# Graph attention on one core: 16-bit projection operands, turns of h between the units of k, and the transposes of the probabilities moved next to the scores

## The reference

```python
h = jnp.maximum(_layernorm(x, axis=-1), 0.0)
q = _split_heads(h @ Wq + bq)
k = _split_heads(h @ Wk + bk)
v = _split_heads(h @ Wv + bv)
scores = jnp.einsum('bhqd,bhkd->bhqk', q, k) / jnp.sqrt(HD)
scores = scores + beta * adj_e
scores = jnp.where(adj_e > 0, scores, -9000000000000000.0)
probs = jax.nn.softmax(scores, axis=-1)
out = jnp.einsum('bhqk,bhkd->bhqd', probs, v)
return x + out.transpose(0, 2, 1, 3).reshape(B, N, D)
```

## Time and profile before

| | |
|---|---|
| median of 3 runs | 1162.26 us (1161.06 to 1162.73) |
| the profiled execution | 1160.99 us, span 1159.1 us |
| busy of the span | PE 94%, PE weight loads 78%, DVE 84%, ACT 77%, POOL 50% |
| granted PE clock, mean | 0.974 of full speed |

### The profile page before, as it was taken

One profiled execution on the slowest core, in us unless ns is written; L12 is line 12 of the kernel. 1 busy time (PEld: TensorE's weight loads), 2 busy tenths in 40 slices (PEclk: granted clock), 3 DMA queues, 4 the chain that ended last, 5 costly groups with the idle time before them and its releaser, 6 DMA issues. The chain is left out here.

```text
span 1159.1 us, 33776 instructions
## 1 busy us (share of the span) xinstructions
PE 1089.7 (94%) x10959; PEld 902.9 (78%) x10959; DVE 972.2 (84%) x4343; ACT 891.0 (77%) x2343; POOL 578.6 (50%) x756
## 2 busy tenths in 40 slices
PE   4899999999999999999999999999999999999986
PEld 2778878888878888787888887888888788888764
DVE  6578888888888888898888888888889888888865
ACT  2377888788787888787888878788877888887865
POOL 3735464454555454546545455545454554545331
PEclk9999999999999999999999999999999999999965
DMA  4444434554434455444455443445544444543320
GB/s 145 116 123 123 110 105 123 140 147 126 120 98 123 130 140 136 120 111 113 119 137 147 130 116 100 122 128 139 145 115 109 114 119 134 147 126 98 98 70 28
DMA packets 91038, 138.79 MB, mean 120 GB/s; under 512 B 15600, under 2 KB 66288, under 8 KB 90864
## 3 DMA queue, kind: packets, MB, share of 16 engines
q1 hardware_dynamic: 90336, 135.85, 43.7%
q10 hardware_dynamic: 528, 0.79, 0.2%
HBM read 35.91 MB, written 25.17 MB: 53 GB/s over the span
## 5 line engine op out<-in xcount | busy, mean ns | idle before, releaser
L523 ACT ACTIVATE probs<-biased,neg_max 128x128 f32<-128x128 f32 x1536 | 491.9, 391 | 222.8 <-DVE neg_max L638 186.0
L435 PE MATMUL ps_p<-hT,w 128*128 128x512 f32 x1728 | 527.1, 423 | 5.2 <-DVE qT L619 2.5
L644 DVE TENSOR_TENSOR pT<-ps_t,pT 128x512 f16<-128x512 f32 x384 | 262.9, 685 | 141.3 <-ACT pT L548 141.0
L334 POOL TENSOR_TENSOR on<-on,xb 128x384 f32<-128x384 f32 x128 | 129.2, 1009 | 471.8 <-DVE on L659 392.9
L638 DVE CUSTOM_DVE_ANT_0 biased<-ps_s,mask 128x128 f32<-128x128 f32 x1536 | 352.0, 285 | 6.3 <-PE ps_s L456 4.3
L435 PEld LDWEIGHTS ps_p<-hT,w 128*128 128x128 f32 x1728 | 294.2, 192 | 53.4 <-DVE hT L609 7.3
L435 PE MATMUL ps_p<-w,hT 128*128 128x384 f32 x1152 | 270.2, 357 | 30.4 <-DVE hT L609 30.4
L464 PE MATMUL ps_t<-ident,probs 128*128 128x128 f32 x1536 | 237.8, 279 | 3.1 <-ACT probs L523 1.5
L464 PEld LDWEIGHTS ps_t<-ident,probs 128*128 128x128 f32 x1536 | 193.9, 143 | 43.8 <-ACT probs L523 7.1
L548 ACT ACTIVATE pT<-ps_t 128x512 f16<-128x512 f32 x384 | 220.5, 574 | 1.2 <-PE ps_t L464 1.2
L435 PEld LDWEIGHTS ps_p<-w,hT 128*128 128x128 f32 x1152 | 186.8, 189 | 37.6 <-DVE hT L609 37.5
(11 more groups left out here) (62 smaller groups left out, 1034.9 us busy)
## 6 DMA issues: line engine op xcount, KB each, us to landing
q_st<-qT SPq DMA_DIRECT2D x384, 96.0 KB, 2.2
k_st<-kT SPq DMA_DIRECT2D x384, 96.0 KB, 2.2
out<-on SPq DMA_DIRECT2D x128, 192.0 KB, 2.1
xs<-in_x SPq DMA_DIRECT2D x31, 768.0 KB, 4.8
adjs<-in_adj SPq DMA_DIRECT2D x32, 256.0 KB, 5.1
xs<-in_x ACTq DMA_DIRECT2D x1, 768.0 KB, 7.6
k_st<-in_L_gnn_Wq SPq DMA_DIRECT2D x1, 576.0 KB, 5.9
k_st<-in_L_gnn_Wk SPq DMA_DIRECT2D x1, 576.0 KB, 9.2
```

Of the source, the lines that this page charges most:

```text
L334: pool.tensor_tensor(on[:, j % 2, :], on[:, j % 2, :], xb[:, par, j, :], ALU.add).then_inc(added, 1)
L435: mm = pe.matmul(dst, stationary, moving, start=m == 0, stop=m == MMS - 1)
L523: act.activation(probs[:, odd, i, :], biased[:, odd, i, :], ACT.Exp, bias=neg_max[:, odd, i:i + 1], scale=-1.0).then_inc(exp_done, 1)
L644: dve.tensor_tensor(pT[:, odd, 1], ps_t[odd][:].rearrange("p (h q) -> p h q", q=N), pT[:, odd, 0], ALU.subtract).then_inc(p_low_done, 1)
```

## The change

1. `w` and `hT` become FP16. To keep small values within the format, h is made smaller by SHRINK = 4 (in the variance that goes into the reciprocal root) and the weights are made larger by 4.
2. The units become q0 q1 q2 k0 turn0 k1 turn1 k2 turn2 v0 v1 v2 v3.
3. The projection work of a slot is one piece, and `turn_probs` comes ahead of it, right behind the scores.
4. On DVE, `moments` and `variance` run for two graphs in slot 0 and two in slot 1, no longer one in each of slots 0 to 3.
5. On POOL, `rstd_of` and `normalise` move ahead of `add_x(s - 2, 2)` and `add_bias(s, 2)`.

```diff
+SHRINK = 4.0
...
-    UNITS = ([("q", c) for c in range(CH)] + [("k", c) for c in range(CH)]
-             + [("v", 0), ("v", 1), ("turn", 0), ("v", 2), ("turn", 1), ("v", 3), ("turn", 2)])
+    UNITS = ([("q", c) for c in range(CH)] + [(kind, c) for c in range(CH) for kind in ("k", "turn")]
+             + [("v", j) for j in range(G)])
...
+    QK_AT = {o: [u for u in UNITS if u[0] in "qk"].index(unit) for o, unit in enumerate(UNITS) if unit[0] in "qk"}
...
-    HALVES = 2 * SLOTS
-    PIECES = [[] for _ in range(HALVES)]
+    PIECES = [[] for _ in range(SLOTS)]
...
-        w = sb("w", [P, 2, CH, 3 * D], F32R)
+        w = sb("w", [P, 2, CH, 3 * D], FP16)
...
-        hT = sb("hT", [P, 2, 2, CH, TOK], F32R)
+        hT = sb("hT", [P, 2, 2, CH, TOK], FP16)
...
-                pool.tensor_scalar(var_eps[:], mean_var[:, :, 1], EPS, None, ALU.add).then_inc(eps_added, 1)
+                pool.tensor_scalar(var_eps[:], mean_var[:, :, 1], SHRINK * SHRINK, SHRINK * SHRINK * EPS, ALU.mult,
+                                   ALU.add).then_inc(eps_added, 1)
...
+                if 0 <= s <= STEPS - 2:
+                    rstd_of(s + 1)
+                    normalise(s + 1, 1 - par)
                 if older:
                     add_x(s - 2, par, 2)
                 if proj:
                     add_bias(s, par, 2)
-                if 0 <= s <= STEPS - 2:
-                    rstd_of(s + 1)
-                    normalise(s + 1, 1 - par)
...
                     if scored:
                         scores(*scored, (u - LAG) % 2)
-                    if proj:
-                        piece(s, par, 2 * u, ahead)
                     if turning:
                         turn_probs(turning[0], (u - LAG - 1) % 2)
                     if proj:
-                        piece(s, par, 2 * u + 1, ahead)
+                        piece(s, par, u, ahead)
                     if valued:
                         values_of(*valued, (u - LAG) % 2)
...
-                act.activation(w[:, 0, :, W_COLS[n]], w_raw[:, :, W_COLS[n]], ACT.Copy).then_inc(w_high, 1)
+                act.activation(w[:, 0, :, W_COLS[n]], w_raw[:, :, W_COLS[n]], ACT.Copy, scale=SHRINK).then_inc(w_high, 1)
...
-                    if ahead and u < G:
-                        moments(s + 1, 1 - par, u)
+                    if ahead and u < 2:
+                        for j in range(2 * u, 2 * u + 2):
+                            moments(s + 1, 1 - par, j)
...
-                    if ahead and u < G:
-                        variance(s + 1, u)
+                    if ahead and u < 2:
+                        for j in range(2 * u, 2 * u + 2):
+                            variance(s + 1, j)
```

More of the change, by code:

```diff
@@ L61, in graph_attention_kernel @@
     TOTAL = sum(a[2] for a in ATOMS)
-    HALVES = 2 * SLOTS
-    PIECES = [[] for _ in range(HALVES)]
+    PIECES = [[] for _ in range(SLOTS)]
     done = 0
     for o, m, cost in ATOMS:
-        runs = PIECES[(2 * done + cost) * HALVES // (2 * TOTAL)]
+        runs = PIECES[(2 * done + cost) * SLOTS // (2 * TOTAL)]
         if runs and runs[-1][0] == o:
@@ L74, in graph_attention_kernel @@
     BANK = [[(o + par) % PB for o in range(NB)] for par in range(2)]
-    ENDED = [[o for o, a, b in PIECES[2 * u] + PIECES[2 * u + 1] if UNITS[o][0] == "turn" or b == MMS]
-             for u in range(SLOTS)]
+    ENDED = [[o for o, a, b in PIECES[u] if UNITS[o][0] == "turn" or b == MMS] for u in range(SLOTS)]
     x_v = x.rearrange("(s j) t d -> s t j d", j=G)
@@ L408, in bank_free @@
                 else:
-                    wait(pe, qk_low, QK * before + last + 1)
+                    wait(pe, qk_low, QK * before + QK_AT[last] + 1)
             def turn(s, bank, c):
@@ L437, in project, with piece @@
                     mm.then_inc(proj_done, 1)
-            def piece(s, par, half, ahead):
-                for o, first, end in PIECES[half]:
+            def piece(s, par, u, ahead):
+                for o, first, end in PIECES[u]:
                     if UNITS[o][0] != "turn":
@@ L609, in turn_low @@
                 dve.scalar_tensor_tensor(out=hT[:, par, 1, c, :], in0=bank[:], scalar=0.0,
-                                         in1=hT[:, par, 0, c, :].bitcast(F32), op0=ALU.max,
+                                         in1=hT[:, par, 0, c, :], op0=ALU.max,
                                          op1=ALU.subtract).then_inc(h_low, 1)
@@ L616, in low_part @@
                 bank = ps_p[BANK[par][o]]
-                dve.wait_ge(qk_high, QK * s + o + 1)
+                dve.wait_ge(qk_high, QK * s + QK_AT[o] + 1)
                 dst, b = (qT, 0) if kind == "q" else (kT, 1)
@@ L724, in weights_low @@
                 dve.wait_ge(w_high, n + 1)
-                dve.tensor_tensor(w[:, 1, :, W_COLS[n]], w_raw[:, :, W_COLS[n]], w[:, 0, :, W_COLS[n]].bitcast(F32),
-                                  ALU.subtract).then_inc(w_low, 1)
+                dve.scalar_tensor_tensor(out=w[:, 1, :, W_COLS[n]], in0=w_raw[:, :, W_COLS[n]], scalar=SHRINK,
+                                         in1=w[:, 0, :, W_COLS[n]], op0=ALU.mult, op1=ALU.subtract).then_inc(w_low, 1)
             turn_low(0, 0, ps_h[0], 0)
```

## The result

| | before | changed |
|---|---|---|
| median of 18 runs each | 1161.55 us (1160.42 to 1162.73) | 1163.67 us (1163.07 to 1164.26) |
| ratio | | 1.002, 95% interval [1.0013, 1.0026] |
| span of the profiled execution | 1159.1 us | 1162.2 us |

The changed kernel is slower by 2.1 us, 1.5 to 3.0 by the interval. The forecast was slower by 4.6. The direction held; the size was twice too large.

What follows compares the result with a forecast made beforehand. Bound: a closed DVE-ACT loop of 2.79 us a slot, not PE. Per step, gains 0.59 and losses 0.77 net +0.17; 30 steps give +5.1, less 0.5 at the start, +4.6: 1167 us, own range 1164 to 1171, 8 in 10 1153 to 1177.

Steps and rivals of the forecast that it cites:

- Rival (a): PE is the bound, saving its stall and some pace, 2.6 us a step: 1084 us; chance 0.05.
- (e): PE's clock falls to 1.2 GHz: 1.4 us per slot hit, +50 if one in ten is; chance 0.05.
- 16-bit parts at nothing: f16 projections save PE between 0 and 3.2 us a step, hidden behind the DVE-ACT loop: 0.
- -0.06 and -0.14: Gains per step in us: 0.06 in slots 0 and 1, 0.14 in slot 11, where PE's late scores go.
- estimate of 1.7 us of PE per step: PE time saved by f16 projections, from 216 ns by the skill page against the trace's 230 at 512 columns; hidden.
- Transposes next to the scores: turn_probs on PE waits some tenths for exps each slot, with over a us of cover: 0.
- Paired moments: A pair in slots 0 and 1 takes 1.2 us; both stay at 2.79, slot 2 falls 3.21 to 2.85.
- Rival (d): Paired moments in slots 0 and 1 don't overlap: +8.4 us more, 1175; chance 0.12.
- Turns between the units of k: DVE's pile in slot 7 costs +0.60 us a step, the bank wait moved to slot 6 another +0.17.
- (b): The pile in slot 7 costs nothing while the gains stand: -18 us, 1144; chance 0.15 for all or part.
- (c): The pile in slot 7 is right, the bank wait isn't: about 0, with the start 1162; chance 0.16.
- The start: First step: low part of q2 on DVE ends about 0.5 us earlier; -0.5 us, between -2 and +1.

Runs made afterwards that it cites:

- e3_f32parts: The changed kernel with w and hT back in F32R, SHRINK kept: 1166.70 us, ratio 1.0062 to the kernel before.
- e10_turns_first_swap: The kernel before with turn_probs right behind the scores and p_high ahead of exps on ACT: 1114.73 us, ratio 0.9617 to the kernel before.
- e2_f16only: The kernel before with only w and hT in FP16 and the factor SHRINK, all orders as before: 1153.43 us, ratio 0.9947.
- e6_before_swap: The kernel before with p_high moved ahead of exps in ACT's order, nothing else: 1158.14 us, ratio 0.9984.
- e11_old_units: The changed kernel with the units back in their old order, turns between those of v: 1153.46 us, ratio 0.9949 to the kernel before.
- e1_mask6: The changed kernel with mask_linked moved from slot 7 to slot 6: 1144.22 us, ratio 0.9868 to the kernel before.
- e4_pairs: The kernel before with only moments and variances paired in slots 0 and 1: 1158.61 us, ratio 0.9992.
- e7_swap_mask6: The changed kernel with p_high ahead of exps on ACT and mask_linked in slot 6: 1069.11 us, ratio 0.9218 to the kernel before.

## Why the prediction was right in its direction and wrong in its size

**The bound: right.** The loop through DVE and ACT sets the pace, not PE. PE's projections, added up from start to start, take some 17.5 us of a step where they took 21.1, and the step didn't fall; f32r in the new order cost 5 us instead of 50; and one exchange on ACT that opens the loop gave 73 us on the changed kernel. Rival (a) is out. So is (e): both pages show the same granted clock in every slice of the steps (the line PEclk), 0.974 and 0.976 in the mean.

**16-bit parts at nothing: right about the pace, not about the first matmul of a group.** Behind the bank wait they give 0.1 us a step, 3 us over 30 steps (`e3_f32parts`; by the ratios 5, with an error of 2), and 0.19 a step or 5.7 us in the old order, mostly in slots 11 and 1. The prediction had a part of that in its -0.06 and -0.14. The estimate of 1.7 us of PE per step doesn't follow from its own 230 and 216 ns, which give some 1.1; the projections of `e3_f32parts` in fact take 2.5 us more of PE than the changed kernel's. Nothing in the sum hung on it.

**Transposes next to the scores: right**, 0.9994. That run keeps the half pieces; the single piece was only run together with the rest. PE's wait for the exps came as foretold and cost nothing.

**Paired moments: right.** Slots 0 and 1 at 2.79, slot 2 from 3.21 to 2.84. Rival (d) is out: 1.20 us for a pair.

**GpSimd's order at nothing: nothing speaks against it.** The slots above add up to the step without a term of its own, but no run changed it alone.

**Turns between the units of k: right in kind, 0.07 too dear.** Slot 7 was put at 3.39 and 0.17 for the bank wait, 3.56; it is 3.48. PE resumed at T + 1.58, as said, but the scores came at T + 2.33 instead of 2.40 (515.66 - 513.33): 0.75 us after the resumption, where 0.82 was put in and f32r takes 0.89. The gains were some 0.06 too large as well: slot 4 rose from 2.75 to 2.79, for which there was no term, and slot 1, read at 2.85, is 2.80 in every second step. The two errors cancel, and that is luck. The net of +0.17 a step, 5.1 us, is what the trace shows. Rivals (b) and (c) are out.

**The start: this is the term that failed.** It was put at -0.5. In the profiled executions it is -2.2: that is the lead of the changed kernel at the `p_low` of slot 0 in the second step with attention. Granted clock (third last number) in the 2 us stretches from 60 and 62 us, before:

```profile
60.00:62.00 2.00, 2.00 (x8) 1.33 (x6) 1.79 (x10) 1.46 (x5) 0.00 (x0) 0.71 0.00 0
62.00:64.00 2.00, 2.00 (x9) 1.59 (x9) 1.53 (x11) 1.14 (x4) 0.75 (x3) 0.50 0.01 4
```

and after:

```profile
60.00:62.00 2.00, 1.88 (x14) 1.07 (x12) 1.90 (x11) 2.00 (x7) 2.00 (x4) 1.00 0.00 0
62.00:64.00 2.00, 2.00 (x18) 1.49 (x16) 2.00 (x5) 1.20 (x3) 0.78 (x1) 1.00 0.32 75
```

PE's wait before the first scores, before and after:

```profile
59.64 0.38 PE L456 MATMUL ps_s<-k_st,q_st 96*128 96x128 f16 x4 [2.53 <-DMA k_st<-kT]
```

```profile
58.05 0.38 PE L458 MATMUL ps_s<-k_st,q_st 96*128 96x128 f16 x4 [1.02 <-DMA k_st<-kT]
```

The queue of SP in the first step, after, against the earlier trace rows:

```profile
38.20 7.56 SPq L249 DMA_DIRECT2D q_st<-qT  x12
...
48.23 7.51 SPq L249 DMA_DIRECT2D k_st<-kT  x12
```

Two things came on top of the 0.6 us by which the q spread is issued earlier (38.20 against 38.81). Its twelve issues took 7.56 us instead of 9.07, and the k spread began 1.0 us earlier (48.23 against 49.20). The first scores, which wait for it, came at 58.05 instead of 59.64. And before, PE stood 2.5 us for that DMA and was then granted half its clock, 1.2 GHz, so that the first `p_low` came at 65.60; after, PE stood 1.0 us, the clock stayed at 2.4 GHz, and it came at 62.98. From the first scores to the first `p_low` that is 5.96 us against 4.93, so the clock is worth some 1.0 us. The prediction priced the order of DVE's instructions and took neither the queue behind them nor the clock.

The other profiles say which part of the change does what, as far as it goes. The paired moments alone bring the first `p_low` to 63.37 with the clock at full speed; the kernel with only the transposes moved, which leaves them single, has it at 65.53 with the clock at half. So the pairing is enough for most of it. It isn't the only way: `e10_turns_first_swap` keeps the moments single, and there PE stands 1.0 us, the clock stays full and the first `p_low` is at 63.48. Half the clock is granted behind the first scores in the four profiles in which PE stood 2.0 to 3.0 us before them (`e2_f16only` and `e6_before_swap` are the other two), and in none of the other ten, where it stood 1.5 us at most. And the twelve issues of q take 7.6 us in the seven kernels with the new unit order and 8.2 to 9.1 in the seven with the old one, `e11_old_units` with 8.32 among them: the shorter issues go with the order of the units, not with the pairing. Why they do wasn't settled.

**The sum** was +5.1 - 0.5. The two profiled executions are 3.1 us apart: +5.0 for 29 steps and +0.4 in the last two, less 2.2 at the start. The medians are 2.1 apart. The missing 1.0 comes from which executions were profiled: the profiled execution of the kernel before is 0.6 under its median, that of the changed one 0.4 over. Taken as a remainder the start would be 2.1 - 5.1 = -3.0, and -2.1 to -3.6 by the interval; in the experiments with the paired moments and the loop closed the same remainder is only -1.0 to -1.6 (`e1_mask6`, `e3_f32parts`, `e4_pairs`, `e11_old_units`), each with an error of some 1.5 us. So the start was mis-sized by 1.7 us as the traces show it, of a net of 4.6. With the right start the same sum would have been +2.9; the rest of the way to 2.1 is within what those remainders scatter, and stays open.

## What to carry to other kernels

When several engines are busy 77 to 94% and each waits for another, look for a closed loop through their in-order queues and read it where the other work is gone; here the tail gave 2.79 us a slot outright. Then price an edit slot by slot as the larger of the loop and the engine's queue: what fits in the loop's slack is free (a mask of 0.68 us in slot 6), the same instruction in a full slot costs some 18 us. And try the loop itself first: with it closed a faster PE was worth 5 or 6 us, with it open 38.

## What the runs showed of the hardware

- A projection matmul of 512 columns is 0.233 us start to start within a row in f32r and 0.216 in f16, and its weight load takes 189 and 98 ns. The larger difference is at the head of each group: from the first matmul's start to the second's it is 0.32 us in f32r (median of 414 groups before and of 246 in `e3_f32parts`) and 0.216 in f16.
- Opening the loop put PE on the path in the tail, where the clock is low. In `e7_swap_mask6` the granted clock is 0.50 from 1036 to 1046 us, and a slot of the tail is 2.96 us, over the 2.79 of the closed loop:

```profile
1041.81 1.12 PE L466 MATMUL ps_t<-ident,probs 128*128 128x128 f32 x4 [1.08 <-ACT probs L523]
...
1042.96 0.60 ACT L548 ACTIVATE pT<-ps_t 128x512 f16<-128x512 f32 x1 [1.21 <-PE ps_t L466]
```

  Four transposes take 1.12 us there, against 0.60 at full clock, and ACT stands for them. In the tail of the kernel before, at the same clock of 0.50, four transposes take 1.12 us too, but there ACT has the exps to do meanwhile, and the slot stays at 2.79.
- The same twelve DMA issues of q on SP took 7.56 to 9.07 us in the first step, by the kernel.
